# Turning quantized rows by DMA instead of TensorE, with the unpacking on GpSimd, in a cross-attention and FFN kernel

## The reference

```python
def fake_quant(x, scale, zp):
    q = jnp.clip(jnp.round(x / s + z), QMIN, QMAX)      # 0 .. 255
    return (q - z) * s

x = x + jnp.matmul(fake_quant(_layernorm(x)), fake_quant(ctx))   # first layer
# second layer, on xf = _layernorm(x)
w = top-2 of softmax(xf @ W_router.T), renormalized
lora_out = einsum('ter,eor,te->to', xf @ lora_A, lora_B, w) * SCALING
x = x + xf @ W_base.T + b_base + lora_out
```

## Time and profile before

| | |
|---|---|
| median of 3 runs | 991.64 us (991.61 to 991.65) |
| the profiled execution, device time | 990.91 us |
| its span, first to last instruction | 989.2 us |
| busy: TensorE, VectorE, ScalarE, GpSimd | 958.8, 794.6, 429.1, 146.8 us |
| granted TensorE clock | 1.00 of full speed over the whole span |

### The profile page before, as it was taken

One profiled execution on the slowest core, in us unless ns is written; L12 is line 12 of the kernel. 1 busy time (PEld: TensorE's weight loads), 2 busy tenths in 40 slices (PEclk: granted clock), 3 DMA queues, 4 the chain that ended last, 5 costly groups with the idle time before them and its releaser, 6 DMA issues.

```text
span 989.2 us, 15078 instructions
## 1 busy us (share of the span) xinstructions
PE 958.8 (97%) x5829; PEld 525.3 (53%) x5829; DVE 794.6 (80%) x1471; ACT 429.1 (43%) x466; POOL 146.8 (15%) x184
## 2 busy tenths in 40 slices
PE   2999999999999999999999999999999999999998
PEld 1766666666699444444444444444444444444444
DVE  7998988989717887997875887757889788798786
ACT  4878887755533435554443552213232323322310
POOL 3645444455100000000000000000000000000000
PEclk9999999999999999999999999999999999999999
DMA  9967676877443337867665664168533143242220
GB/s 373 371 228 297 265 275 268 295 303 267 151 139 133 108 102 227 269 213 231 228 229 171 202 232 103 57 220 287 176 109 129 69 144 118 80 151 92 87 75 33
DMA packets 62312, 185.66 MB, mean 188 GB/s; under 512 B 6896, under 2 KB 19488, under 8 KB 56096
## 3 DMA queue, kind: packets, MB, share of 16 engines
q1 hardware_dynamic: 58648, 174.18, 49.5%
q0 software_dynamic: 1280, 2.12, 2.1%
q10 hardware_dynamic: 2312, 8.39, 2.1%
HBM read 151.07 MB, written 33.60 MB: 187 GB/s over the span
## 4 chain that ended last, share of the span: by engine, by line
PE 86%; DVE 0%; issue 0%
PE pair L1877 34%; PE pair L1901 29%; PE pair L1714 13%; PE pair L1839 5%; PE pair L1849 4%; PE pair L1913 1%; PE pair L1722 0%; PE pair L1819 0%; PE pair L1693 0%; PE pair L1734 0%; DVE sq L1563 0%; DVE xt L1018 0%; DVE u L1565 0%; PE pair L1728 0%; PE pair L1813 0%; PE pair L1738 0%
## 5 line engine op out<-in xcount | busy, mean ns | idle before, releaser
L1877 PE MATMUL pair<-x2p,w_p 128*128 128x512 f16 x1536 | 337.0, 379 | 0.0
L1877 PEld LDWEIGHTS pair<-x2p,w_p 128*128 128x128 f16 x1536 | 150.3, 98 | 180.4
L1714 PE MATMUL pair<-q1T,ctx_q 128*128 128x342 f16 (+2 forms) x1584 | 228.6, 305 | 4.8 <-DVE xt L1018 2.8
L1714 PEld LDWEIGHTS pair<-q1T,ctx_q 128*128 128x128 f16 x1584 | 152.7, 97 | 75.1 <-issue 3.8
L1901 PE MATMUL pair<-x2p,w_slot 128*128 128x512 f16 x744 | 163.8, 379 | 0.0
L836 ACT ACTIVATE sq<-pair,lsc 128x512 f32<-128x512 f32 x64 | 43.5, 681 | 210.2 <-PE pair L1849 174.3
L1638 POOL TENSOR_SCALAR ctx_u<-ctx_f,par 128x512 uint8<-128x512 f32 x128 | 114.2, 905 | 109.5 <-DMA ctx_f<-in_ctx 88.4
L1901 PEld LDWEIGHTS pair<-x2p,w_slot 128*128 128x128 f16 x744 | 72.7, 98 | 87.9
L864 ACT ACTIVATE w_slot<-w_q,usc 128x1024 f16<-128x1024 f32 x32 | 36.5, 1146 | 90.8 <-DVE usc L1469 27.2
L1901 PE MATMUL pair<-x2p,x2p 128*128 128x512 f16 x336 | 74.3, 379 | 0.0
L734 ACT ACTIVATE xt<-xt,colt 128x1024 f32<-128x1024 f32 x32 | 36.7, 1146 | 55.1 <-DVE xt L1018 55.1
(11 more groups left out here) (223 smaller groups left out, 1112.8 us busy)
## 6 DMA issues: line engine op xcount, KB each, us to landing
ctx_f<-in_ctx SPq DMA_DIRECT2D x32, 1024.0 KB, 7.4
xt<-in_xT SPq DMA_DIRECT2D x32, 512.0 KB, 4.6
w_r<-in_w_n SPq DMA_DIRECT2D x32, 512.0 KB, 7.3
w_f<-in_w_t SPq DMA_DIRECT2D x32, 512.0 KB, 5.9
w_q<-in_w_t SPq DMA_DIRECT2D x32, 512.0 KB, 4.9
outT<-u SPq DMA_DIRECT2D x63, 256.0 KB, 2.7
rows<-in_x SPq DMA_DIRECT2D x15, 1024.0 KB, 9.8
x_kept<-xt ACTq DMA_DIRECT2D x16, 512.0 KB, 4.3
```

The source lines that it names most:

```text
L1714: ins = M.matmul(bank[at % RING][:, 0:w], ctx_q[n % NQ][:, k, :], q1T[b][:, k, t0:t0 + w], start=(k == 0), stop=(k == KT - 1))
L1877: M.matmul(base_bank(m)[:, :], w_p[j % 2][wh][:, k, :], x2p[0][:, k, xh, t], start=(k == 0 and q == 0), stop=(k == KT - 1 and q == 2))
```

## The change

For batch 1, `turn(T)` and `ln_copy(T)` go. In their place SP starts a DMA that transposes the words of `q1u` (128x1024, 16 bits, 256 KB) into a new buffer `q1t`, and GpSimd unpacks that into `q1T[1]` (`row_copy_of`, four instructions for each tile). Batch 0 stays on TensorE and ScalarE. ScalarE converts all context tiles from the fifth (tile 4) on; VectorE keeps tiles 2 and 3. The load of `ar_f`, whose place overlaps `q1t`, moves from step 15 to step 18; `stat_sums(0)` moves behind the last chunks of steps 16 and 17; ScalarE converts tile 17 ahead of `col_add_of(14)`.

```diff
-ON_ACT = [0, 1] + list(range(4, STEPS, 2))
+ON_ACT = [0, 1] + list(range(4, STEPS))
...
+            def turn_rows(T):
+                wait_bytes(sp, T)
+                if T - TT >= 2:
+                    sp.wait_ge(q1T_copied1, T - TT - 1)
+                sp.dma_start_transpose(q1t[T % 2][:, :, :], q1u[1][T % 2][:, :].bitcast(U16)).then_inc(q1_moved[T % 2], 16)
...
             load_ctx(5)
+            turn_rows(TT)
             load_rows(TT + 2)
             for n in range(3, STEPS):
                 load_xt(n)
                 if n + 3 < STEPS:
                     load_ctx(n + 3)
+                if n == 3:
+                    turn_rows(TT + 1)
+                if n - 3 in BYTES_AT:
+                    turn_rows(BYTES_AT[n - 3])
                 if n in LOAD_AT:
                     load_rows(LOAD_AT[n])
-                if n == JT - 1:
+                if n == JT + 2:
+                    sp.wait_ge(q1T_copied1, TT)
                     sp.dma_start(ar_f[:, :, :], ar).then_inc(ar_landed, 16)
...
             for n in range(STEPS):
+                if n == JT - 2:
+                    ctx_act_of(n + 3)
                 col_add_of(n)
...
-                if n == 1:
-                    ln_copy(TT)
-                if n + 3 in ON_ACT and n + 3 > 4:
+                if n + 3 in ON_ACT and n + 3 > 4 and n != JT - 2:
                     ctx_act_of(n + 3)
-                if n == 2:
-                    ln_copy(TT + 1)
                 if n in BYTES_AT:
                     ln_bytes_of(BYTES_AT[n])
-                if n - 1 in BYTES_AT:
-                    ln_copy(BYTES_AT[n - 1])
...
+            def row_copy_of(T):
+                t = T - TT
+                pool.wait_ge(q1_moved[T % 2], 16 * (t // 2 + 1))
+                turned = q1t[T % 2][:, :, :].rearrange("p m t -> p (m t)").bitcast(U8).rearrange("p (m t e) -> p m e t", m=PAIRS, e=2)
+                dst = q1T[1][:, :, t * P:(t + 1) * P].rearrange("p (m e) t -> p m e t", e=2)
+                for q in range(4):
+                    c = slice(2 * q, 2 * q + 2)
+                    ins = G.tensor_scalar(dst[:, c, :, :], turned[:, c, :, :], LO1, None, ALU.add)
+                ins.then_inc(q1T_copied1, 1)
...
             for n in range(STEPS):
                 ctx_bytes_of(n)
+                if n in (6, 7):
+                    if n == 6:
+                        pool.wait_ge(par_step, 3)
+                    row_copy_of(TT + n - 6)
+                if n - 4 in BYTES_AT:
+                    row_copy_of(BYTES_AT[n - 4])
                 if n in POOL_AT:
                     row_bytes_of(POOL_AT[n])
...
                 chunk(n, 0)
-                if n == 3:
-                    turn(TT)
-                if n == 4:
-                    turn(TT + 1)
                 chunk(n, 1)
...
                 chunk(n, 2)
-                if n - 2 in BYTES_AT:
-                    T = BYTES_AT[n - 2]
-                    turn(T)
```

More of the change, by code:

```diff
@@ L7 @@
 I32 = mybir.dt.int32
+U16 = mybir.dt.uint16
 U8 = mybir.dt.uint8
@@ L146, in xattn_ffn @@
         ar_f = place("ar_f", [P, KT, AR], FP32, ROW_AT[1] + 2 * D * 4 + 2 * D)
+        q1t = [place(f"q1t{s}", [P, PAIRS, P], U16, ROW_AT[1] + 2 * D * 4 + 2 * D + s * D) for s in range(2)]
         ctx_f = [place(f"ctx_f{s}", [P, KT * P], FP32, C + s * KT * P * 4) for s in range(2)]
@@ L267, in xattn_ffn @@
         q1_turned = sem("q1_turned")
+        q1_moved = [sem(f"q1_moved{s}") for s in range(2)]
         q1T_copied = sem("q1T_copied")
+        q1T_copied1 = sem("q1T_copied1")
         bound_step = sem("bound_step")
@@ L708, in ln_bytes_of @@
                 act.wait_ge(ln_scale, g + 1)
-                if T % TT >= 2:
+                if b and T - TT >= 2:
+                    act.wait_ge(q1_moved[T % 2], 16 * ((T - TT) // 2))
+                elif T % TT >= 2:
                     act.wait_ge(q1_turned, T - 1)
@@ L1149, in fold_of @@
                 if t == 0:
-                    dve.wait_ge(q1T_copied, ROWS)
+                    dve.wait_ge(q1T_copied1, TT)
                 V.tensor_tensor(folded[:, :, c], q1T[1][:, 0:HALF, c], q1T[1][:, HALF:KT, c], ALU.add).then_inc(fold_step, 1)
@@ L1645, in row_bytes_of @@
                 pool.wait_ge(ln_scale, g + 1)
-                if T % TT >= 2:
+                if b == 0 and T >= 2:
                     pool.wait_ge(q1_turned, T - 1)
@@ L1686, in turn @@
                 wait_bytes(pe, T)
-                if T >= TT:
-                    pe.wait_ge(q1T_copied, T)
-                elif T >= 2:
+                if T >= 2:
                     pe.wait_ge(q1T_copied, T - 1)
@@ L1709, in chunk @@
                 t0, w, need = pieces(n)[c]
-                pe.wait_ge(q1T_copied, b * TT + need)
+                pe.wait_ge(q1T_copied1 if b else q1T_copied, need)
                 if at >= RING:
@@ L1786, in _ @@
                     chunk(n, 1)
-                    pe.wait_ge(q1T_copied, ROWS)
+                    pe.wait_ge(q1T_copied1, TT)
                     turn_bound(1)
-                    stat_sums(0)
                     chunk(n - 1, 2)
                     chunk(n, 2)
+                    stat_sums(0)
                     continue
                 chunk(n, 0)
-                if n == 3:
-                    turn(TT)
-                if n == 4:
-                    turn(TT + 1)
                 chunk(n, 1)
```

1 line of the change is left out of this document (removed).

## The result

The changed kernel takes 1029.47 us (median of 4 runs, 1027.95 to 1030.91) against 991.64 us (991.61 to 991.66, 4 runs). The ratio is 1.0381, 95% interval 1.0363 to 1.0399: slower by 37.8 us. The sign was forecast; the size, 3.2 us with a range up to 1001, was not. In the runs further down, one launch of x15 stood apart at 1126.43 us with a granted clock of 0.857, and is left out of its figures.

A forecast was written before the change was run, and what follows sets the result against it. Up to about 170 us the row-tile loads were taken to pace the kernel, TensorE being busy for 958.8 of 989.2 us. Transposes less turns, +2.6, and GpSimd's copies, +0.6, gave +3.2 us: median 994.8 us, range 988.5 to 1001.

The forecast's parts named there:

- The sign: Whole kernel: slower by over 0.2%, given 0.48, from the forecast case at 0.38 and dear transposes at 0.10.
- GpSimd's copies: GpSimd's queue near 120 us: copies of 3.1 us make ScalarE 2.7 us late, mostly hidden; 0.6 us taken.
- Eight turns at 0.45 us are 3.6 us: TensorE, attention stage: the time it saves by no longer transposing batch 1's row tiles, 3.6 us.
- so 0.9 us is certain if nothing is late behind it: TensorE: two turns, at 141.48 and 155.87, lie behind its last wait for VectorE; their 0.9 us is saved.
- VectorE's conversions, up to -1.5 us: VectorE: dropped conversions bring statistics forward, at most 1.29 us at tile 11 and 0.24 at tile 13.
- ScalarE, nothing: ScalarE: loses copies of 1.948 us and gains 14 conversions of 1.987 us, trading one for one; no effect.
- So SP waits no longer than before, but 256 KB more pass the full DMA engines ahead of the row tile.: SP's queue: each transpose delays the row loads behind it by t; with the turns' 0.9 the sum is 5t - 2.43.
- t: Time one transpose holds the DMA engines ahead of a row tile: taken as 1.0 us, bounds 0.62 to 2.7.
- The 10.5 us: Skill-based estimate for one transpose as eight crossbar blocks of 1309 ns in series; another skill section implied 0.7 us.
- The third number in that sum: GpSimd's block near 120 us, 115.7 + 1.0 + 3.1 + 3.0 = 122.8: the 1.0 is the transpose behind context tile 13.
- Dear transposes: Rival on the DMA transposes: t of 2.7 us or more adds 11.1, time 1003 and above; chance 0.10.

The follow-up runs named there:

- x15: x14 with the context conversions split between ScalarE and VectorE as in the kernel before; 995.37 us.
- x12: Kernel before with one TensorE transpose instead of eight for each of batch 1's row tiles, ScalarE's copies kept; 992.42 us.
- x5: Kernel before with ScalarE converting all context tiles from the fifth on, the turns and row copies left as they were; 993.34 us.
- x1: Kernel before with the eight DMA transposes added ahead of the row loads, nobody reading their output; 998.89 us.
- x9: x1 with each idle transpose replaced by five tiny copies, so SyncE still issues but almost no bytes move; 1000.21 us.
- x8: x1 with each idle transpose replaced by a plain copy of the same 256 KB in the same queue place; 996.28 us.
- x7: x1 with the idle transposes issued behind the row load of the same step instead of ahead of it; 993.98 us.
- x13: Changed kernel with GpSimd's copy written as a multiplication by 1 and an addition instead of an addition alone, same result; 1016.08 us.
- x4: Changed kernel with GpSimd's copies of tiles 10 to 14 two steps later and tile 15 one step later, same instructions; 1003.45 us.
- x14: Changed kernel with GpSimd's copies as multiplication and addition and placed later, and the transposes issued behind the row loads; 993.82 us.
- x11: Changed kernel with GpSimd's copies placed later as in x4 and the transposes issued behind the row loads; 1002.55 us.

## Why the prediction was right about the sign and wrong about the size

Of the sum of +3.2 us, 2.6 were for the transposes ahead of the row loads less the turns, and 0.6 for GpSimd's copies. By the runs the first part was too small by a few microseconds, and the second by about 30. So the sign, given a chance of 0.48, came true in the main by a mechanism that the sum held for next to nothing, and that is in good part luck.

1. **"Eight turns at 0.45 us are 3.6 us", "so 0.9 us is certain if nothing is late behind it".** Wrong, shown by x12: seven eighths of the turns taken away gave +0.9 us, not -3.1. The 0.9 was argued from the chain, which names the turns at 141.48 and 155.87; but a chain shows where the time passed, not what would have followed without them. Without them the chain of x12 comes from VectorE's `acc`, and TensorE's L1722 starts no earlier than before.
2. **VectorE's conversions, up to -1.5 us; ScalarE, nothing.** The first was not there: x5 gave +1.5 us for both together. For ScalarE the account was of sums (2.0 us for 1.95), and the sums hold; the wait of VectorE for ScalarE grew by 10.5 us, most of it harmless.
3. **"So SP waits no longer than before, but 256 KB more pass the full DMA engines ahead of the row tile."** Half wrong. At t = 1.0 this term, without the turns' 0.9, is 5t - 1.53 = 3.5 us; x1 measured 7.1, which is t = 1.7. That lies inside the bounds taken (0.62 to 2.7), but t is not what it was said to be: x9 has the loss without the bytes, x8 a good half of it without the long issue, x7 little (1.9) with both. The missing row in the sum was SyncE's time for an issue, 1.35 to 3.75 us in the changed kernel against the 0.33 of the earlier trace rows. The text had rightly placed the transpose ahead of the row load; it priced only what flows, not what issues. The 10.5 us that it gives as an estimate for eight blocks in series did not come: a transpose landed after 3.2 to 9.6 us. Against the other estimate there, 0.7 us, stands the 1.7 of x1, a part of which is the issue.
4. **GpSimd's copies: "Most of that is hidden in VectorE's wait of 1.35 us and in the DMA backlog. Between 0 and 2.7 I take 0.6."** This is the step that failed: about 31 of the 37.8 us. Two errors lie in it. The copy was priced 4 x 0.771 = 3.1 us by the nearest instruction in shape; it takes 6.2, and x13 shows that this is worth 13.4 us. And the lateness was put down once, at one place. It comes back each round, since ScalarE's bytes of the next row tile stand behind the conversion of the context tile that stands behind GpSimd's wait. The text named every link ("ScalarE is 2.7 us late there, and its `ln_bytes_of(13)`, `hi_of` and then SP's row load behind it") and did not ask whether the last one leads back to the first. x4 shows that the loop is the cause: its order alone returned 26.0 us. The third number in that sum, a transpose landing 1.0 us behind context tile 13, was right. That tile was issued at 125.08 us in the changed kernel and the transpose at 125.51; the DMA view gives, to landing:

```profile
ctx_f<-in_ctx SPq DMA_DIRECT2D x1, 1024.0 KB, 7.8
...
q1t<-q1u SPq DMA_TRANSPOSE x1, 8.5
```

Both are late together, since both are issued late in the ring.
5. **The rivals.** "Dear transposes" gave 1003 and above, nearest in size by another mechanism. The view that would show it was named: "a `ctx_q` releaser ahead of TensorE would say that I priced GpSimd's queue too low" is the 39.5 us of ScalarE's wait, with 11.1 us at TensorE. ScalarE's wait was foretold near 120 us and stands at 121.13.

The account of the 37.8 us, in the order in which the experiments took it away: the copy's pair of operations 13.4 (x13); its place in GpSimd's order and SyncE's order together 22.3 (x14 against x13); what stays 1.9 (the sets' times of before differ by 0.3). Taken in the other order the place alone is 26.0 (x4), SyncE's order nothing that x11's spread lets one tell and the pair 8.7 (x14 against x11), so the parts overlap. TensorE's clock fell as well: granted 0.78 of 2.4 GHz on average from 100 to 125 us, so at 1.2 GHz for a part of it, where it was busy for 16.6 of 25 us. Its attention matmuls were busy for 239.6 us in place of 228.6. Between 56 and 204 us the chain holds no piece of TensorE, so by this view the slower matmuls followed from the ring and did not pace it; no run measured that apart. A third `q1t` buffer was not tried; by the trace it would not matter, as the copy that frees the buffer for the transpose at 125.51 us had ended at 98.4.

## What to carry to other kernels

Where work is moved to an engine that has room, draw the waits of one round as a circle and add the times around it: if an engine's queue now waits for something that its own next output helps to make, the sum of the latencies is the pace, however idle each engine looks. First ask what the moved step stands in front of, on the new engine and on the queue that feeds it; here one step put two places later was worth 26.0 us, more than any duration. And a freed microsecond of the busiest engine may be worth nothing until an experiment such as x12 shows that nobody else is next in line.
